# Rounding and absolute sums of the weights moved to ScalarE, and the instruction orders of a decoder layer rewritten

## What is computed

```
x = layernorm(x + attention(x, Wq, Wk, Wv, Wo))        # 16 heads of 64, 4 key/value heads, rope, alibi, softmax
x = layernorm(x + cross(x, ctx, ctx, cell))            # layernorm with gain and bias ahead of each of 4 projections,
                                                       # 16 heads of 16, windows of 64 with the one before,
                                                       # masked where the cell numbers differ
x = layernorm(x + ffn(x))                              # silu(gate) * up, then down; inner size 1024
# ffn weights: w -> clip(round(w / mean|w|), -1, 1) * mean|w|  (ternary); ffn activations: rounded to 8 bits per token
```

## Time and profile before

| | |
|---|---|
| median of 3 runs | 2292.14 us |
| the profiled execution's own time | 2293.73 us |
| its span, from the first to the last instruction | 2291.6 us |
| TensorE clock granted, mean over the span | 0.979 |
| iterations of `BODY` | 27 |

### The profile page before, as it was taken

One profiled execution on the slowest core, in us unless ns is written; L12 is line 12 of the kernel. 1 busy time (PEld: TensorE's weight loads), 2 busy tenths in 40 slices (PEclk: granted clock), 3 DMA queues, 4 the chain that ended last, 5 costly groups with the idle time before them and its releaser, 6 DMA issues. The chain is left out here.

```text
span 2291.6 us, 57972 instructions
## 1 busy us (share of the span) xinstructions
PE 2147.3 (94%) x19370; PEld 1649.6 (72%) x19370; DVE 1954.5 (85%) x7981; ACT 1695.3 (74%) x4738; POOL 1434.2 (63%) x1678
## 2 busy tenths in 40 slices
...
DMA packets 85397, 74.64 MB, mean 33 GB/s; under 512 B 18544, under 2 KB 79344, under 8 KB 85104
## 3 DMA queue, kind: packets, MB, share of 16 engines
...
...
## 5 line engine op out<-in xcount | busy, mean ns | idle before, releaser
L1379 POOL TENSOR_TENSOR prob<-prob,precs 128x512 f32<-128x512 f32 x512 | 525.9, 1044 | 218.7 <-DVE precs L1014 216.0
L1287 ACT ACTIVATE prob<-prob,nmax 128x256 f32<-128x256 f32 x1024 | 509.3, 503 | 155.2 <-DVE nmax L1007 155.2
L1007 DVE CUSTOM_DVE_ANT_0 prob<-bank,alibi 128x256 f32<-128x256 f32 x1024 | 371.4, 419 | 13.5 <-PE bank L715 12.4
L611 PE MATMUL bank<-ident,prob 128*128 128x128 f32 x2048 | 315.9, 277 | 5.7 <-ACT pT L1294 5.0
L1311 ACT ACTIVATE px<-px,nmx 128x128 f32<-128x128 f32 x1024 | 315.1, 409 | 4.8 <-DVE nmx L1116 4.8
L1294 ACT COPY pT<-bank 128x512 f32<-128x512 f32 x512 | 300.3, 587 | 12.1 <-PE bank L611 12.0
L611 PEld LDWEIGHTS bank<-ident,prob 128*128 128x128 f32 x2048 | 236.7, 141 | 80.9 <-issue 43.3
L734 PE MATMUL bank<-pT,v_sb 128*64 128x256 f32 x2048 | 250.5, 386 | 5.9 <-DVE qq_lo L998 5.9
L1116 DVE CUSTOM_DVE_ANT_0 px<-bank,mask 128x128 f32<-128x128 f32 x1024 | 225.5, 285 | 29.1 <-PE bank L794 26.2
L623 PE MATMUL bank<-w_hi,x_hi 128*128 128x512 f32 (+1 forms) x512 | 199.2, 389 | 23.6 <-POOL x_lo L1359 16.6
L734 PEld LDWEIGHTS bank<-pT,v_sb 128*64 128x64 f32 x2048 | 142.7, 137 | 101.0 <-issue 45.6
...
## 6 DMA issues: line engine op xcount, KB each, us to landing
...
kx<-k_sin SPq DMA_DIRECT2D x256, 32.0 KB, 2.0
...
```

The lines of the kernel that those rows point to most:

```text
L611: last = nc.tensor.transpose(bank[:, n * P:(n + 1) * P], src, ident[:])
L1007: v.tensor_tensor_reduce(out=prob[:, (2 * p + q) % SLOTS, c, :], in0=psum[SCORES[c]][:, q * L:(q + 1) * L], in1=alibi[:, p % 2, :], scale= ...
L1287: nc.scalar.activation(prob[:, (2 * p + q) % SLOTS, c, :], prob[:, (2 * p + q) % SLOTS, c, :], ACT.Exp, bias=nmax[:, i:i + 1], scale=-1.0, ...
L1379: g.tensor_tensor(prob[:, n % SLOTS, :, :], prob[:, n % SLOTS, :, :], precs[:, 2 * n:2 * n + 2].unsqueeze(2).to_broadcast([P, 2, L]), ALU. ...
```

## The change

Three things.

1. The roundings to the high part (`w_hi`, the three cross weights, `wo_hi`) and the three sums of absolute values move from DVE to ACT, each with a semaphore of its own (`w_rounded`, `crossed_rounded`, `w_sums`). The sums are ACT activations `Abs` with an accumulator; their elementwise output goes into the tile `kx`, after `Wo` has been split out of it. PE's matmul over the sums and POOL's clearing of `kx` wait for `w_sums`.
2. `loads` 0 on SP asks for the cross weights, `ropex` and `pen` without a wait; only the four bias loads wait for the split of the first weights (tile `hh`).
3. `HEAD`, `BODY` and `TAIL` have new orders on all engines. The steps and their instructions are the same.

The core of the diff (left out are the parts of the tables that the text does not speak of, and the renumbering of `P_CROSSED`, `PRE_DVE` and of the waits that follow from it):

```diff
 BODY = {
     "sp": [
-        (2, 'load_ctxT'), (2, 'load_xtok'), (1, 'load_cell'), (4, 'store'), (0, 'load_xT'), (1, 'load_ctx'),
-        (2, 'load_vs'), (2, 'fill_kx'),
+        (2, 'load_cell'), (3, 'load_vs'), (2, 'load_ctxT'), (3, 'fill_kx'), (2, 'load_xtok'), (2, 'load_ctx'),
+        (0, 'load_xT'), (4, 'store'),
     ],
     "pe": [
-        (4, 'HT', 0), (3, 'TX', 1, 1), (3, 'SX', 3), (2, 'T', 13), (3, 'OX', 0), (3, 'TX', 2, 0), (1, 'kT'),
-        (3, 'TX', 2, 1), (4, 'D', 0), (2, 'T', 14), (4, 'HT', 1), (3, 'TX', 3, 0), (1, 'qT', 1), (4, 'D', 1),
-        (3, 'TX', 3, 1), (1, 'S', 0), (3, 'OX', 1), (1, 'Q', 0, 2), (3, 'BX', 0), (2, 'T', 15), (1, 'S', 1), (2, 'KV', 0),
-        (2, 'O', 3), (1, 'T', 0), (3, 'BX', 1), (1, 'Q', 1, 2), (3, 'NO'), (1, 'T', 1), (1, 'S', 2), (3, 'PO'),
-        (2, 'W', 1), (2, 'KV', 1), (1, 'T', 2), (1, 'V'), (1, 'qT', 2), (1, 'T', 3), (2, 'KXT'), (1, 'S', 3), (1, 'O', 0),
-        (1, 'T', 4), (3, 'XQ'), (0, 'K'), (3, 'G', 0), (3, 'U', 0), (2, 'NX'), (1, 'T', 5), (1, 'S', 4), (3, 'G', 1),
-        (3, 'U', 1), (2, 'QX'), (1, 'qT', 3), (1, 'T', 6), (3, 'G', 2), (3, 'U', 2), (0, 'Q', 0, 1), (1, 'T', 7),
-        (1, 'S', 5), (1, 'O', 1), (3, 'G', 3), (1, 'T', 8), (2, 'QXT'), (3, 'U', 3), (0, 'Q', 1, 1), (1, 'T', 9),
-        (1, 'S', 6), (2, 'SX', 0), (1, 'W', 0), (1, 'T', 10), (2, 'SX', 1), (0, 'qT', 0), (2, 'TX', 0, 0), (1, 'T', 11),
-        (1, 'S', 7), (2, 'TX', 0, 1), (2, 'SX', 2), (1, 'O', 2), (2, 'TX', 1, 0), (1, 'T', 12),
+        (4, 'HT', 1), (1, 'S', 0), (1, 'qT', 1), (3, 'TX', 3, 0), (4, 'D', 1), (3, 'TX', 3, 1), (2, 'T', 15), (1, 'S', 1),
+        (3, 'OX', 1), (1, 'Q', 0, 2), (3, 'BX', 0), (2, 'O', 3), (1, 'T', 0), (3, 'BX', 1), (1, 'Q', 1, 2), (3, 'NO'),
+        (1, 'T', 1), (1, 'S', 2), (1, 'T', 2), (3, 'PO'), (2, 'W', 1), (2, 'KV', 0), (1, 'V'), (1, 'qT', 2), (1, 'T', 3),
+        (1, 'S', 3), (2, 'KV', 1), (1, 'O', 0), (1, 'T', 4), (2, 'NX'), (0, 'K'), (3, 'XQ'), (1, 'T', 5), (1, 'S', 4),
+        (3, 'G', 0), (3, 'U', 0), (2, 'QX'), (1, 'T', 6), (1, 'qT', 3), (3, 'G', 1), (3, 'U', 1), (0, 'Q', 0, 1),
+        (2, 'KXT'), (1, 'T', 7), (3, 'G', 2), (3, 'U', 2), (1, 'S', 5), (1, 'O', 1), (1, 'T', 8), (3, 'G', 3),
+        (3, 'U', 3), (2, 'QXT'), (0, 'Q', 1, 1), (1, 'T', 9), (1, 'S', 6), (2, 'SX', 0), (1, 'W', 0), (1, 'T', 10),
+        (2, 'TX', 0, 0), (2, 'SX', 1), (0, 'qT', 0), (2, 'TX', 0, 1), (1, 'T', 11), (1, 'S', 7), (2, 'SX', 2),
+        (1, 'O', 2), (2, 'TX', 1, 0), (1, 'T', 12), (3, 'HT', 0), (2, 'TX', 1, 1), (2, 'SX', 3), (2, 'OX', 0),
+        (2, 'TX', 2, 0), (1, 'T', 13), (0, 'kT'), (3, 'D', 0), (2, 'TX', 2, 1), (1, 'T', 14),
     ],
...
 HEAD = {
...
     "pe": [
-        (0, 'first', 0), (0, 'first', 1), (0, 'V'), (0, 'K'), (0, 'Q', 0, 1), (0, 'Q', 1, 1), (0, 'first', 2),
-        (0, 'prep', 1), (0, 'prep', 2), (0, 'prep', 3), (0, 'qT', 0), (0, 'qT', 1), (0, 'Q', 0, 2), (0, 'Q', 1, 2),
-        (0, 'kT'), (1, 'K'), (0, 'prep', 5), (0, 'KV', 0), (0, 'S', 0), (0, 'S', 1), (0, 'qT', 2), (0, 'T', 0),
-        (0, 'T', 1), (0, 'wo_ready'), (0, 'S', 2), (0, 'T', 2), (0, 'T', 3), (0, 'S', 3), (0, 'O', 0), (0, 'T', 4),
+        (0, 'first', 0), (0, 'first', 1), (0, 'K'), (0, 'Q', 0, 1), (0, 'first', 2), (0, 'prep', 1), (0, 'prep', 2),
+        (0, 'Q', 1, 1), (0, 'prep', 3), (0, 'qT', 0), (0, 'kT'), (0, 'S', 0), (0, 'S', 1), (0, 'V'), (0, 'qT', 1),
+        (0, 'Q', 0, 2), (0, 'Q', 1, 2), (0, 'prep', 5), (0, 'T', 0), (0, 'T', 1), (0, 'T', 2), (0, 'S', 2), (0, 'qT', 2),
+        (0, 'T', 3), (0, 'S', 3), (0, 'O', 0), (0, 'T', 4), (0, 'T', 5), (0, 'S', 4), (1, 'K'), (0, 'T', 6), (0, 'qT', 3),
...
     "dve": [
         (0, 'first', 0), (0, 'first', 1), (0, 'first', 2), (0, 'prep', 0), (0, 'tables', 0), (0, 'K'), (0, 'Q', 0, 1),
-        (0, 'Q', 1, 1), (0, 'prep', 1), (0, 'prep', 2), (0, 'prep', 3), (0, 'prep', 4), (0, 'qT', 0), (0, 'wo_split'),
-        (0, 'CS'), (0, 'qT', 1), (0, 'Q', 0, 2), (0, 'Q', 1, 2), (0, 'prep', 5), (0, 'prep', 6), (0, 'kT'),
-        (0, 'prep', 7), (0, 'tables', 1), (0, 'S', 0), (0, 'R', 0), (0, 'R', 1), (0, 'S', 1), (0, 'R', 2), (1, 'K'),
+        (0, 'prep', 1), (0, 'prep', 2), (0, 'prep', 3), (0, 'Q', 1, 1), (0, 'prep', 4), (0, 'tables', 1), (0, 'qT', 0),
+        (0, 'kT'), (0, 'S', 0), (0, 'S', 1), (0, 'wo_split'), (0, 'R', 0), (0, 'R', 1), (0, 'R', 2), (0, 'R', 3),
+        (0, 'qT', 1), (0, 'Q', 0, 2), (0, 'prep', 6), (0, 'Q', 1, 2), (0, 'S', 2), (0, 'prep', 7), (0, 'qT', 2),
+        (0, 'R', 4), (0, 'R', 5), (0, 'S', 3), (0, 'prep', 8), (0, 'R', 6), (0, 'R', 7), (0, 'O', 0), (1, 'K'),
...
     "act": [
-        (0, 'X'), (0, 'V'), (0, 'tables', 0), (0, 'Q', 0, 1), (0, 'Q', 1, 1), (0, 'qT', 0), (0, 'qT', 1), (0, 'Q', 0, 2),
-        (0, 'Q', 1, 2), (1, 'X'), (0, 'C'), (0, 'kT'), (0, 'S', 0), (0, 'S', 1), (0, 'T', 0), (0, 'qT', 2), (0, 'T', 1),
+        (0, 'first', 0), (0, 'first', 1), (0, 'first', 2), (0, 'X'), (0, 'tables', 0), (0, 'Q', 0, 1), (0, 'Q', 1, 1),
+        (0, 'prep', 4), (0, 'wo_split'), (0, 'qT', 0), (0, 'kT'), (0, 'S', 0), (0, 'S', 1), (0, 'V'), (0, 'qT', 1),
+        (0, 'Q', 0, 2), (0, 'prep', 5), (0, 'T', 0), (0, 'T', 1), (0, 'T', 2), (0, 'Q', 1, 2), (0, 'S', 2), (0, 'qT', 2),
...
 TAIL = {
...
     "pe": [
...
-        (31, 'KXT'), (30, 'XQ'), (30, 'G', 0), (30, 'U', 0), (31, 'NX'), (30, 'G', 1), (30, 'U', 1), (31, 'QX'),
-        (30, 'G', 2), (30, 'U', 2), (30, 'G', 3), (31, 'QXT'), (30, 'U', 3), (31, 'SX', 0), (31, 'SX', 1),
+        (31, 'O', 3), (30, 'PO'), (31, 'KV', 0), (31, 'KV', 1), (31, 'W', 1), (30, 'XQ'), (31, 'NX'), (30, 'G', 0),
+        (30, 'U', 0), (31, 'QX'), (30, 'G', 1), (30, 'U', 1), (31, 'KXT'), (31, 'QXT'), (30, 'G', 2), (30, 'U', 2),
+        (30, 'G', 3), (30, 'U', 3), (31, 'SX', 0), (31, 'SX', 1), (31, 'TX', 0, 0), (31, 'TX', 0, 1), (30, 'HT', 0),
...
@@ SP
                             sp.dma_start(gb[:].rearrange("p c k -> p (c k)"), a["gb"]).then_inc(gb_loaded, 16)
-                            sp.wait_ge(w_split, 12)
...
-                        for dst, src in later_loads[g]:
+                        for i, (dst, src) in enumerate(later_loads[g]):
+                            if g == 0 and i == 5:
+                                sp.wait_ge(w_split, 3 * KT)
                             sp.dma_start(dst, src).then_inc(later_loaded[g], 16)
@@ DVE
-                    for hi, rawer in ((wkvx_hi, raw_kvx), (wqx_hi, raw_qx), (wox_hi, raw_ox)):
-                        v.tensor_copy(hi[:], rawer).then_inc(pre_dve, 1)
-                    dve.wait_ge(pre_dve, P_CENTRED + 5)
+                    dve.wait_ge(crossed_rounded, 3)
...
-                elif n == 5:
-                    dve.wait_ge(later_loaded[2], 16 * len(later_loads[2]))
-                    for m in range(3):
-                        v.tensor_reduce(wsum[:, m:m + 1], stage[m], AX_X, ALU.add, apply_absolute_value=True).then_inc(pre_dve, 1)
...
-                        dve.wait_ge(first_loaded[i], 16 * KT)
-                        for k in range(KT):
-                            v.tensor_copy(w_hi[:, k, cols], raw_w[k][:, cols]).then_inc(w_split, 1)
                         for k in range(KT):
-                            dve.wait_ge(w_split, 4 * i + k + 1)
+                            dve.wait_ge(w_rounded, KT * i + k + 1)
...
-                        dve.wait_ge(later_loaded[1], 16)
-                        v.tensor_copy(wo_hi[:], raw_wo).then_inc(wo_split, 1)
@@ ACT
+                    if kind == "first":
+                        i, = args
+                        cols = slice(512 * i, 512 * i + 512)
+                        act.wait_ge(first_loaded[i], 16 * KT)
+                        for k in range(KT):
+                            nc.scalar.copy(w_hi[:, k, cols], raw_w[k][:, cols]).then_inc(w_rounded, 1)
+                    elif kind == "wo_split":
+                        act.wait_ge(later_loaded[1], 16)
+                        nc.scalar.copy(wo_hi[:], raw_wo).then_inc(wo_split, 1)
...
+                        if args[0] == 4:
+                            act.wait_ge(pre_dve, P_CENTRED)
+                            for hi, rawer in ((wkvx_hi, raw_kvx), (wqx_hi, raw_qx), (wox_hi, raw_ox)):
+                                nc.scalar.copy(hi[:], rawer).then_inc(crossed_rounded, 1)
+                        elif args[0] == 5:
+                            act.wait_ge(later_loaded[2], 16 * len(later_loads[2]))
+                            act.wait_ge(wo_split, 2)
+                            for m in range(3):
+                                if m > 0:
+                                    act.wait_ge(w_sums, m)
+                                nc.scalar.activation(kx[:].rearrange("p k h n -> p (k h n)"), stage[m], ACT.Abs, accum_out=wsum[:, m:m + 1])\
+                                    .then_inc(w_sums, 1)
```

(12 more changed lines are left out.)

30 lines of the change are left out of this document (17 added, 13 removed), and 329 rows, old and new, of tables (BODY, HEAD, TAIL).

## The result

The changed kernel takes 2252.26 us (median of 4 runs, 2250.7 to 2253.05), the kernel before 2292.56 beside it. The ratio is 0.9822, with a 95% interval of 0.9807 to 0.9836: 40 us faster. The forecast was 2277, 15 us faster, with a range down to 2263. The sign was right; the size was far too small.

A forecast was written before the change was run, and what follows sets the result against it. PE was taken to set the pace of the steady batches, and the chain before the first scores to bound the head. 2293.73 − 10 (head) − 7 (body) + 2 (tail) = 2278.7; less 1.6 is 2277 us, range 2263 to 2291.

The forecast's parts named there:

- −0.87 + 0.15 + 0.45 = −0.27 a batch: Body: PE waits removed, tighter orders elsewhere, late `fill_kx` and the rest; × 27 = −7 us.
- At most 0.9 a batch falls away: Body: cap on PE's removable waits: the longer behind `TX` (0.46), `x` (0.23), `qq_lo` (0.18).
- 0.15 for orders made tighter elsewhere: Body: +0.15 us a batch, as `XQ` follows `NX` and `K`, and `K`, `V`, `Q` share bank 3 with `TX`.
- for this and the rest: Body: +0.45 us a batch for `fill_kx` perhaps landing after PE reaches `SX` 0, and other delays, between 0 and +1.3.
- equal within 0.1: Body: `fill_kx`'s chain of 8.5 us against 8.55 of PE steps between `KXT` and `SX` 0, cover about 0.
- Steps 2 to 5: Head: DVE's rope product −3.8 us, `prep` 1 −8.0, cross split and ffn loads −9.2, first score −31.
- step 6: Head: most of the lead given back; ACT's three sums of 1.9 us end near 63, fourth score −14.6.
- The start stays: 0: Head: PE still starts at 12.45, when POOL's first `x_lo` is done; bound +1.3 us.
- the port-pair rival: Head: DVE's castings alone lengthen POOL's first `x_lo` through shared ports; PE starts 1.7 us sooner, 2275; chance 0.05.
- The sum of 10: Head: −10 us reaches the body, bounds −4 and −15 (lead of the fourth score holds).
- Nearly all of the waits go: Body rival: −0.8 us a batch, −22 in all, fill in time: 2262; chance 0.15.
- The slower one: Body rival: `fill_kx`'s DMAs land after PE reaches `SX` 0; at +0.5 us a batch 2298; chance 0.12.

The follow-up runs named there:

- kxt_first: The changed kernel with `KXT` ahead of `qT` 3 in DVE's list of `BODY`: 2241.5 us, ratio 0.9771 to the kernel before.
- gb_later: The kernel before with DVE's four copies of the gains moved behind `Q`(1,1): 2298.72 us, ratio 1.0026.
- first_on_dve: The changed kernel with the castings of the first weights back on DVE: 2249.61 us, ratio 0.9813 to the kernel before.
- new_body: Code and `HEAD` of the kernel before, with the new `BODY` and `TAIL` and the steps between filled in: 2269.51 us, ratio 0.9891.

## Why the forecast was right or wrong

**The body was mis-sized, and this is the failed step.** "−0.87 + 0.15 + 0.45 = −0.27 a batch" was −0.98: 27 batches of it are 26 us in place of 7.

- "At most 0.9 a batch falls away" took the cap from listed idle time. All of the regular waits went, and the listed ones fell from 1.26 to 0.55 a batch with the two new ones in it. The idle time fell by only 0.50, but PE's busy time, which the sum put at nothing, fell by 0.48: waits are longer than the list shows. kxt_first shows the same on a single wait (0.23 listed, 0.34 gained).
- "Kept: the shorter wait behind `TX`, 0.25" and "0.15 for orders made tighter elsewhere": neither stands in the list after. `SX` 2 waits 0.30 for DVE's maxima, which the walk hadn't seen.
- The fill was priced at 0.45 "for this and the rest"; it costs 0.23 listed and 0.34 by kxt_first. That there is next to no cover was right: with the step 0.55 sooner the wait is gone, with 1.8 later it costs 1.2 to 1.3. But "equal within 0.1" was luck of the batch: the eight issues take 5.14 in the earlier trace rows and 5.9 in the median of ten batches before, which makes the chain some 9.3 against 8.55.

**The head was right step by step and short in its sum.** Steps 2 to 5 came out within 2.5 us, most of the difference being the start (the sums of step 6 ended at 59.2 for 63). "The start stays: 0" was wrong: the port-pair rival (0.05) was right about the start, and PE starts at 10.79. Its cause was only in part "DVE's castings alone", since half of the 1.7 goes with the copies of the gains (gb_later); and what the start is worth at the end is too little to measure (first_on_dve). DVE's fourth score is at 72.82, 18.0 sooner for the 14.6 walked, and the fifth at 82.44, 14.4 sooner (96.83 before), so less was given back than the walk had. At the copy of `V`(3) 17.5 us are left, beyond the bound of 15: PE's idle time up to there is 10.0 less (54.9 and 44.9), as the sum had it, and its busy time is 7.5 less (212.36 and 204.89). Some 1 to 2 us of this is the moved place of `V` (new_body).

The sum of 10 had the later scores "meet PE at half clock". In the windows of 10 us the clock is back sooner. Before:

```profile
70.00:80.00 10.00, 4.58 (x28) 3.30 (x26) 8.39 (x16) 2.08 (x8) 1.21 (x2) 0.50 0.22 72
80.00:90.00 10.00, 7.79 (x44) 6.11 (x44) 5.46 (x23) 6.49 (x21) 6.50 (x8) 0.50 0.00 1
90.00:100.00 10.00, 8.30 (x57) 5.53 (x55) 5.00 (x24) 6.78 (x22) 4.48 (x6) 0.84 0.01 2
```

and after:

```profile
70.00:80.00 10.00, 7.63 (x62) 5.71 (x60) 9.86 (x16) 4.88 (x14) 6.02 (x5) 0.91 0.10 29
80.00:90.00 10.00, 7.98 (x51) 6.10 (x51) 7.98 (x31) 6.36 (x21) 5.99 (x6) 0.83 0.00 0
90.00:100.00 10.00, 9.25 (x79) 7.91 (x81) 5.54 (x20) 6.97 (x20) 9.65 (x9) 1.00 0.09 26
```

In windows of 1 us, PE is at 1.2 GHz before until 93.1 without a break from about 62 on; after, until 71.8 and once more from 82.0 to 85.5. That the clock is the cause of the rest of these 7.5 us is argued from the windows, not tried.

**The moved work was given credit that belongs to the order.** Steps 3 to 5 priced castings, sums and loads as relief of the path. Undone one by one they cost nothing that the whole time can show; done without the new orders they bring nothing. In the new orders the whole of the moved work brings 7 us, in the head.

One row was misread: ACT's 0.642 for 512 elements is shorter than the 0.69 of the DVE operation beside it, so those two rows don't agree in direction with a rule that sends plain work to VectorE. The like pair is a casting of 512 elements, 0.62 on ACT and 0.42 on DVE, and it does.

```profile
6.88 0.42 DVE L957 CAST w_hi<-px 128x512 fp32r<-128x512 f32 x1
```

**The tail** lost 4 for the 2 forecast, at the end of its range, and not by the forecast's mechanism. The keys of batch 31 are late, but the wait of 1.83 for them replaces one of 2.62, and PE's idle time doesn't grow; the 4 us are busy time, most of it at a lower clock. That the number still lies in the range is luck.

**The rivals.** "Nearly all of the waits go" (0.15, 2262) was the nearest, and its size was too small for the same reason as the forecast's. The slower one didn't happen, by a margin of 1.3 us a batch (66.05, where 67.03 + 0.3 decides).
